# Adjacency tiles transposed by DMA instead of TensorE, column sums by later passes on ScalarE

## What is computed

```python
h = relu(layernorm(x));  mask = (adj > 0)
agg = mask @ h / max(sum(mask, axis=1), 1)
x = x + relu(concat(h @ W_self + b_self, agg @ W_nb + b_nb) @ W_comb + b_comb)
state = h = relu(layernorm(x));  A = adj as float
for _ in range(5):
    a_in  = A   @ (state @ in_W.T + in_b)
    a_out = A.T @ (state @ out_W.T + out_b)
    a = concat(a_in, a_out, state)
    r = sigmoid(a @ r_W.T + r_b);  z = sigmoid(a @ z_W.T + z_b)
    hh = tanh(concat(a_in, a_out, r * state) @ h_W.T + h_b)
    state = (1 - z) * state + z * hh
x = x + tanh(state @ o1_W.T + o1_b) @ o2_W.T + o2_b
```

## Time and profile before

| | us |
|---|---|
| median of 3 runs | 1241.61 (1240.56 to 1242.62) |
| the profiled execution | 1241.1 |
| its span, first to last instruction | 1239.3 |
| mean granted TensorE clock | 0.996 |
| TensorE matmuls busy | 1223.2 (99%) |
| TensorE weight loads busy | 591.1 (48%) |
| VectorE busy | 758.8 (61%) |
| ScalarE busy | 285.3 (23%) |
| GpSimd busy | 15.4 (1%) |
| DMA, mean rate | 146 GB/s |

### The profile page before, as it was taken

The page is one execution under the profiler, slowest core; times in us unless marked ns, Lnnn a source line. Parts: engine busy times, 40 slices in busy tenths (PEclk is TensorE's granted clock), DMA queues, the critical chain, the costliest instruction groups (busy, mean ns, idle before and its releaser), DMA issues.

```text
span 1239.3 us, 12868 instructions
## 1 busy us (share of the span) xinstructions
PE 1223.2 (99%) x4872; PEld 591.1 (48%) x4872; DVE 758.8 (61%) x1275; ACT 285.3 (23%) x556; POOL 15.4 (1%) x15
## 2 busy tenths in 40 slices
PE   8999999999899999999999999999999999999998
PEld 5666654444344444444444444444444444444445
DVE  6677734787884374387447348726834863662674
ACT  5756200022222021032112103301201330210122
POOL 4000000000000000000000000000000000000000
PEclk9999999999999999999999999999999999999999
DMA  9444643950007803810750570082075029016202
GB/s 328 161 162 171 250 174 141 342 237 0 1 0 287 290 1 111 305 60 0 281 194 1 198 277 1 34 335 106 1 276 199 1 102 345 29 56 216 89 1 68
DMA packets 44506, 180.61 MB, mean 146 GB/s; under 512 B 3489, under 2 KB 13474, under 8 KB 29346
## 3 DMA queue, kind: packets, MB, share of 16 engines
q1 hardware_dynamic: 43440, 176.04, 39.3%
q0 software_dynamic: 720, 3.67, 0.8%
q10 hardware_dynamic: 290, 0.14, 0.0%
HBM read 144.71 MB, written 35.13 MB: 145 GB/s over the span
## 4 chain that ended last, share of the span: by engine, by line
PE 88%; DVE 1%; issue 0%; DVEq 0%
PE bank L344 87%; PE bank L514 1%; DVE LF L1196 0%; DVE GR L1343 0%; PE bank L464 0%; DVE GR L1346 0%; DVE H L1092 0%; DVE AT L1049 0%; PE bank L412 0%; DVE DR L1060 0%; DVE fresh_S L1180 0%; DVE fresh_L L1178 0%; DVE res L1454 0%; DVE GR L1356 0%; DVE stat L987 0%
## 5 line engine op out<-in xcount | busy, mean ns | idle before, releaser
L344 PE MATMUL bank<-slot,LF 128*128 128x512 f16 x1792 | 389.5, 379 | 1.7 <-DVE LF L1196 1.7
L344 PEld LDWEIGHTS bank<-slot,LF 128*128 128x128 f16 x1792 | 175.2, 98 | 212.1 <-issue 4.5
L344 PE MATMUL bank<-X,W 128*128 128x512 f32 x384 | 180.5, 592 | 0.0
L344 PE MATMUL bank<-XT,W 128*128 128x512 f32 x288 | 135.3, 592 | 0.0
L344 PEld LDWEIGHTS bank<-X,W 128*128 128x128 f32 x384 | 72.5, 190 | 88.0 <-issue 86.9
L344 PE MATMUL bank<-AT,SN 128*128 (+1 forms) x256 | 97.1, 379 | 0.0
L344 PE MATMUL bank<-A,SN 128*128 (+1 forms) x256 | 97.0, 379 | 0.0
L1242 DVE TENSOR_TENSOR u_buf<-bank,m_buf 128x512 f32<-128x512 f32 x16 | 11.1, 691 | 134.0 <-PE bank L344 134.0
L344 PEld LDWEIGHTS bank<-XT,W 128*128 128x128 f32 x288 | 54.7, 190 | 68.9 <-issue 68.2
L764 ACT ACTIVATE m_buf<-bank 128x512 f32<-128x512 f32 x46 | 27.4, 595 | 232.0 <-PE bank L344 232.0
L344 PE MATMUL bank<-DR,work 128*128 128x512 f16 x256 | 67.1, 386 | 1.8 <-DVE DR L1060 1.6
(11 more groups left out here) (216 smaller groups left out, 1411.0 us busy)
## 6 DMA issues: line engine op xcount, KB each, us to landing
slot<-quad_d SPq DMA_DIRECT2D x112, 1024.0 KB, 5.3
WG<-in_adj SPq DMA_DIRECT2D x32, 512.0 KB, 4.2
quad_d<-AT SPq DMA_DIRECT2D x12, 1024.0 KB, 5.0
quad_d<-A SPq DMA_DIRECT2D x12, 1024.0 KB, 8.6
quad_d<-spare SPq DMA_DIRECT2D x4, 1024.0 KB, 4.0
SN<-in_x SPq DMA_DIRECT2D x2, 1024.0 KB, 10.5
x_d<-SN POOLq DMA_DIRECT2D x4, 512.0 KB, 3.2
x1o<-x_d SPq DMA_DIRECT2D x1, 2048.0 KB, 8.4
```

The costliest lines, as they stand in the source:

```text
L344: return pe.matmul(o, l, r, start=start, stop=stop, skip_group_check=again)
```

## The change

- TensorE's `turn_adj` and both `move_adj` are gone. SP turns a group of four tiles, a converted 512x512 part of A, with four DMA transposes of 128x512 from A to AT, group j behind its conversions and ahead of the load k = 2j+4. Four semaphores, used in turn, count their landing (TURNS).
- Group 4 waits for the last transpose of h and h's low half, since the buffer of h lies where AT is written; groups 8 and 12 wait for the setup and the store of the fused weights. These waits were ScalarE's and VectorE's.
- ScalarE converts further ahead of its loop index: five passes in four turns.
- Column sums: `column_sums` makes 64 passes on ScalarE over AT with accum_out into two scratch tiles, blocks 0 and 1 before out_pq(0), blocks 2 and 3 before out_pq(1).
- diag is split in two; the column diagonals are made after these passes, between VectorE's out_pq(1) and the first quad sums, in WG's place. spread_degrees(1) goes from the first spread to the middle of the third; out_degrees(1) goes between the two quad sums of A and AT, and the fourth spread waits for it.

```diff
+            def turn_adj(j):
+                b, c = j // 4, j % 4
+                sp.wait_ge(conv, 4 * (j + 1))
+                if j == 4:
+                    sp.wait_ge(hT_ready, NB)
+                    sp.wait_ge(h_lo, 4)
+                if j == 8:
+                    sp.wait_ge(setup_done, 1)
+                if j == 12:
+                    sp.wait_ge(st_fused, 16)
+                if j >= TURNS:
+                    sp.wait_ge(at_in[j % TURNS], 64 * (j // TURNS))
+                for q in range(BT):
+                    sp.dma_start_transpose(AT[:, b, BT * c:BT * c + BT, q * P:q * P + P],
+                                           A[:, c, BT * b + q, :]).then_inc(at_in[j % TURNS], 16)
+
             for k in range(2 * 4 * NB):
                 b, c, h = k // 8, k // 2 % 4, k % 2
                 if k >= RING:
                     sp.wait_ge(conv, 2 * (k - RING + 1))
+                if k >= 4 and k % 2 == 0:
+                    turn_adj(k // 2 - 2)
                 sp.dma_start(ring[:, k % RING, :, :], adj_v[b, c, h]).then_inc(ld_ring[k % RING], 16)
...
-                if i + LEAD < NT * NB:
-                    turn_adj(i + LEAD)
...
-            spread_degrees(1)
             spread(0, 11, NT - BT)
             pe.wait_ge(sn_hi, NB)
             pe.wait_ge(sn_lo, NB)
             spread(0, NT - BT, NT).then_inc(agg_done, 1)
+            spread(1, 0, NT).then_inc(agg_done, 1)
+            pe.wait_ge(pq_act, 2)
+            pe.wait_ge(pq_dve, 2)
+            spread(2, 0, 8)
+            pe.wait_ge(pq_act, 4)
+            pe.wait_ge(pq_dve, 4)
+            pe.wait_ge(diag_ready, 2)
+            spread_degrees(1)
+            spread(2, 8, NT).then_inc(agg_done, 1)
             pe.wait_ge(deg_out, 2 * NB)
-            for b in range(1, NB):
-                if b > 1:
-                    pe.wait_ge(pq_act, 2 * (b - 1))
-                    pe.wait_ge(pq_dve, 2 * (b - 1))
-                spread(b, 0, NT).then_inc(agg_done, 1)
+            spread(3, 0, NT).then_inc(agg_done, 1)
...
+            def column_sums(b):
+                for m in range(NT):
+                    i = NT * b + m
+                    if i >= 2:
+                        act.wait_ge(deg_sum, i - 1)
+                    copy(trash[i % 2], AT[:, b, m, :], accum_out=degT[:, m, b:b + 1]).then_inc(deg_sum, 1)
...
+            converted = 4
             for i in range(NT * NB):
-                k = 2 * (i // 4 + 1) + i % 4 // 2
-                if i == 0:
-                    move_adj(0)
-                if k < 8 * NB:
-                    convert(k, i % 2)
+                while converted < min(4 * NT, 5 + i + (i + 1) // 4):
+                    convert(converted // 2, converted % 2)
+                    converted += 1
...
             for b in range(NB):
+                if b < 2:
+                    column_sums(2 * b)
+                    column_sums(2 * b + 1)
                 out_pq(b)
...
             def make_mask(i):
                 b, m = i // NT, i % NT
-                if i % 2 == 0:
-                    dve.wait_ge(at_act, i // 2 + 1)
-                else:
-                    dve.wait_ge(at_dve, i // 2 + 1)
+                j = i // 4
+                if i % 4 == 0:
+                    dve.wait_ge(at_in[j % TURNS], 64 * (j // TURNS + 1))
...
             out_pq(0)
             out_pq(1)
+            dve.wait_ge(deg_sum, NT * NB)
+            link(v.tensor_reduce(degs[:, 1, :], degT[:, :, :], mybir.AxisListType.X, ALU.add))
+            diagonals(1)
             dve.wait_ge(quads_out, 16 * 12)
-            for x in range(2):
-                quad_sums(0, x)
+            quad_sums(0, 0)
+            dve.wait_ge(h2T_ready, NB)
+            out_degrees(1, degT_all)
+            dve.wait_ge(deg_out, 2 * NB)
+            quad_sums(0, 1)
```

More of the change, by code:

```diff
@@ L38 @@
 LEAD = 3
+TURNS = 4
 C_ID, C_ONE, C_END = 0, P, 2 * P
@@ L108, in graph_net @@
         first_XS = at("first_XS", 120 * KB, [P, 4, BN], FP32)
+        trash = [at(f"trash{i}", (202 + i) * KB, [P, BN], FP16)[:, :] for i in range(2)]
         x1o = at("x1o", 96 * KB, [P, NT, D], FP32)
@@ L129, in graph_net @@
         hi_lo = work[:, :].bitcast(FP16).rearrange("p (t s d) -> p t s d", t=NT, s=2)
-        diag = work[:, 8192:16384].bitcast(FP16).rearrange("p (w t n) -> p w t n", w=2, t=NT)
+        diag = [work[:, 8192:12288].bitcast(FP16).rearrange("p (t n) -> p t n", t=NT),
+                WG[:, :, :].rearrange("p k n -> p (k n)")[:, 0:1024].bitcast(FP16).rearrange("p (t n) -> p t n", t=NT)]
         idle16 = work[:, 0:2 * BN].bitcast(FP16)
@@ L180, in graph_net @@
         conv = sem("conv")
-        tr_ready = sem("tr_ready")
-        at_act, at_dve = sem("at_act"), sem("at_dve")
+        at_in = [sem(f"at_in{i}") for i in range(TURNS)]
+        deg_sum = sem("deg_sum")
         mask_ready, mask_used = sem("mask_ready"), sem("mask_used")
@@ L264, in _ @@
                     sp.wait_ge(conv, 2 * (k - RING + 1))
+                if k >= 4 and k % 2 == 0:
+                    turn_adj(k // 2 - 2)
                 sp.dma_start(ring[:, k % RING, :, :], adj_v[b, c, h]).then_inc(ld_ring[k % RING], 16)
-            sp.wait_ge(conv, 4 * NT)
-            sp.wait_ge(at_act, NT * NB // 2)
-            sp.wait_ge(at_dve, NT * NB // 2)
+            turn_adj(4 * NB - 2)
+            turn_adj(4 * NB - 1)
+            for i in range(TURNS):
+                sp.wait_ge(at_in[i], 64 * 4 * NB // TURNS)
             for p in range(2):
@@ L397, in biases @@
                 last.then_inc(setup_done, 1)
-            def turn_adj(i):
-                b, m = i // NT, i % NT
-                pe.wait_ge(conv, 4 * (4 * b + m // 4 + 1))
-                if i == 0:
[L403 to L407, removed]
-                    else:
[L409 to L413, removed]
             def mean_sum(i):
@@ L422, in mean_sum @@
                     pe.wait_ge(w12_out, 1)
+                    pe.wait_ge(id16_ready, 1)
                 if m == 0 and b > 0:
@@ L465, in turn_h2 @@
                 last.then_inc(h2T_ready, 1)
-            for i in range(LEAD):
-                turn_adj(i)
             biases()
@@ L505, in spread_degrees @@
                     last = mm(gate_bank[t // BT][:, (t % BT) * P:(t % BT) * P + P], one16[:, :],
-                              diag[:, w, t, :], True, True)
+                              diag[w][:, t, :], True, True)
                     if t % BT == BT - 1:
@@ L687, in _ @@
             pe.wait_ge(sn_lo, NB - 1)
-            pe.wait_ge(at_act, NT * NB // 2)
-            pe.wait_ge(at_dve, NT * NB // 2)
+            for i in range(TURNS):
+                pe.wait_ge(at_in[i], 64 * 4 * NB // TURNS)
             spread(0, 0, 2)
@@ L872, in _ @@
                 stage()
+            for i in range(TURNS):
+                act.wait_ge(at_in[i], 64 * 4 * NB // TURNS)
             def out_pq(b):
@@ L1114, in _ @@
                     sums(i // NT - 1)
-                if i % 2 == 1:
-                    move_adj(i)
                 if i in LOW_AT:
@@ L1141, in _, with diagonals @@
             dve.wait_ge(conv, 4 * NT)
-            dve.wait_ge(at_act, NT * NB // 2)
             v.tensor_reduce(degs[:, 0, :], degA[:, :, :], mybir.AxisListType.X, ALU.add)
-            v.tensor_reduce(degs[:, 1, :], degT[:, :, :], mybir.AxisListType.X, ALU.add)
             row_stats(range(BT * (NB - 1), NT), BT * (NB - 1))
             variance(range(BT * (NB - 1), NT), BT * (NB - 1))
-            for w in range(2):
+            def diagonals(w):
                 for t in range(NT):
-                    ins = v.tensor_scalar(diag[:, w, t, :], id16[:, :], degs[:, w, t:t + 1], None, ALU.mult)
-            ins.then_inc(diag_ready, 1)
+                    ins = v.tensor_scalar(diag[w][:, t, :], id16[:, :], degs[:, w, t:t + 1], None, ALU.mult)
+                ins.then_inc(diag_ready, 1)
+            diagonals(0)
             newton(BT, NB + 1)
@@ L1162, in _ @@
             turned(NB - 1)
-            dve.wait_ge(h2T_ready, NB)
-            out_degrees(1, degT_all)
-            dve.wait_ge(deg_out, 2 * NB)
             def out_pq(b):
```

21 lines of the change are left out of this document (removed).

## The result

The changed kernel takes 1268.4 us (median of 4 runs, 1266.51 to 1269.6), beside 1242.11 for the kernel before on the same chip: a ratio of 1.0212 (95% interval 1.0194 to 1.0229), so 26 us slower. The forecast was 5 us slower, 1246, with a range of 1230 to 1295. The sign was right, the size was not. The profiled execution has a span of 1267.8 us against 1239.3.

A forecast was written before the change was run, and what follows sets the result against it. TensorE, busy 99%, bounds the kernel. The adjacency stage gains 0.6 us net of stops, the lower clock costs 3.6 and the propagation stage 2.0: 5.0 us slower, 1246 us, range 1230 to 1295.

The forecast's parts named there:

- SP as the bound, slower by over 20 us: Rival for the adjacency stage: SP's transposes and loads outlast TensorE's work per group, slower by over 20 us; chance 0.22.
- What TensorE gives up: Adjacency stage: transposes cost TensorE 0.22 us each, 64 of them 14.1 us; a turn takes 0.97 us instead of 1.19.
- SP's price: Adjacency stage: one DMA transpose of 128x512 holds SP for 1.0 us, with ends of 0.37 and 9.3 us.
- The supply: Adjacency stage: a step with transposes takes 9.9 us, one without 5.9, so 5.3 us a group; TensorE averages 5.8.
- The threshold of the second rival: Adjacency stage: from about 1.4 us a transpose, SP takes 6.3 us a group against TensorE's 5.8; chance 0.22.
- The DMA engines are not the bound: Adjacency stage: 64 transposes at 0.45 us add 29 us to the DMA engines' 0.44 x 108.6 = 48 us.
- The stops: Adjacency stage: TensorE stands about 4 us at turns 30 and 46, together 8 us.
- The first block: Adjacency stage: four groups supplied at 5.3 us against TensorE's 4.8 lose 2 us.
- The lower clock: Adjacency stage: after each of two 4 us stops TensorE runs at a lower clock, costing 3.6 us together.
- A sign of being wrong: Adjacency stage: the prediction is wrong if the three-slot ring of loads runs dry where SP is idle; no size given.
- The propagation stage: Matmuls unchanged; later column sums and stores leave TensorE standing 2.0 us at the first gate group.
- The first rival: Adjacency stage: a transpose holds SP like a plain 128 KB load, 0.58 us or less; kernel 1234 us; chance 0.34.

The follow-up runs named there:

- the mix: Kernel before, with inserted groups of two adjacency loads plus transposes or plain copies, nothing waiting: 6.47 us a group with four transposes, 6.01 one wide, 3.77 copies.
- the two half versions: Kernel before with late column sums, every second group transposed by DMA, load first, buffers exchanged: 1265.9 us; with conversions further ahead and seven DMA groups: 1238.7 us.

## Why the prediction came out as it did

The direction was right, for a mechanism that the forecast had in part and priced too low. The 26 us lie above the 1240 to 1258 that the forecast gave itself; they fall under what it called "SP as the bound, slower by over 20 us", to which it gave 0.22. By its own steps:

- **What TensorE gives up** (0.22 us a tile): right. Two turns in the changed kernel without a stop start their matmuls at 159.64 and 160.62, 0.98 apart.
- **SP's price**, taken as 1.0 us: 1.27, inside the forecast's bounds. The load was taken at its row of before, 0.37; behind transposes it is 0.55 (1.09 for two, SP's timeline), and it lands after 5.1 us (median) instead of 4.2.
- **The supply**, 5.3 us a group: this is the term that was mis-sized. The formula comes near. With the measured values a step with transposes is 5.1 + 0.55 + 5.1 + 1.3 = 12.0 us, one without 6.95, and three groups in 19 us are 6.3 a group; SP's timeline shows 6.4 at best and 6.8 on average. That is above TensorE's 5.8, so nothing is ever caught up, and the stops are longer.
- **The threshold of the second rival** failed. It said that SP is the bound from 1.4 us a transpose, from 4 x 1.4 + 0.7. With two loads at 0.55 it is (5.8 - 1.1) / 4 = 1.18, and 1.27 is above it. What happened is the start of that rival; the forecast thought it 0.13 us away.
- **"The DMA engines are not the bound"** failed. By their share when nothing else runs, a transpose costs them 0.64 us, not the 0.45 of a load of the same size: 64 x 0.64 = 41 us beside 48 of loads, which would still fit into the stage. But between loads it costs more: the mix takes 6.01 us a group with a wide transpose and 3.77 with plain copies, and SP is then held for twice the time that the instruction takes alone. So I can't split the 16 us between plain copies and transposes into SP's part and the engines'; each alone gives a floor of 6.0 to 6.2 us a group.
- **The stops**: two of 4 us at masks 30 and 46 were forecast, 6.46 and 6.95 came. The start was to be 1.5 us late and was 3.0. The first block was to lose 2 us; three stops there (2.37, 2.41, 2.20) make 7.0. The 5.93 us at the first block's sums was missed. The prediction saw that at i = 16 ScalarE waits for these sums, but not that the sums then wait for a load (what it counts there as pieces 25 to 41 are passes, two to a piece): they stand behind a conversion of the piece that SP's hole at group 4 had delayed. With the buffers exchanged this stop is gone.
- **The lower clock** behind two stops, 3.6 us: it followed five of the seven. Of the 39.3 us that the stage lost (25.2 + 14.1), 30.5 are the seven stops and 1.4 are shorter waits for masks (3.1, where the kernel before has 1.7). The 7.4 left is about what the clock cost: from start to start, the work behind the five stops takes some 9.4 us more than the same work at the upper level, and the kernel before has 1.6 of that at the start of its own loop.
- **A sign of being wrong** that the prediction named, a ring that runs dry where SP is idle, came once: SP stood from 52.1 to 58.4 us for turn_h, and ScalarE's wait for the next piece was 9.2 us. The prediction had put this wait into the first block's 2 us.
- **The propagation stage** came out as worked out. Passes follow each other in 0.61 us (0.62 taken, 0.81 as the rival's), VectorE waits 1.48 us for the last of them (1.3 in the forecast's steps, 202.7 to 204.0), 16 diagonals take 2.69 (2.65), and VectorE waits 2.69 us for the stores of A's sums. The stop at the first gate group is 1.77 us, where 2.0 was forecast, and the version with the late sums alone shows 1.79. That its time is not longer by as much means that the 2.0 in the sum was right as a stop and too high as a price.

VectorE's timeline after shows these steps:

```profile
228.56 0.22 DVE L1391 TENSOR_REDUCE degs<-degT 128x16 f32<-128x64 f32 x1 [1.48 <-ACT trash L773]
228.81 2.69 DVE L1142 TENSOR_SCALAR WG<-id,degs 128x128 f16<-128x128 f16 x16
...
258.29 1.23 DVE L1213 TENSOR_TENSOR first_XT<-first_X,first_X 128x1024 f32<-128x1024 f32 x1 [2.69 <-DMA quad_d<-A]
```

The first rival (a transpose as cheap for SP as a load, 1234) is out by the 1.27 us, against 0.60 for a plain copy in the same form. The Trainium skill, page "Advanced Engine Details and Errata", section "X-Bar Transpose (TRN2)", has transpose DMAs as fast as regular ones; the runs here don't agree (0.64 against 0.39 us of the engines, and twice SP's time).

Where the expected gain went is thus known in its parts: 14.1 us were given up on TensorE as forecast. About 16 us were lost because these are transposes and not copies. About 24 more (10 over the kernel before, and the 14.1 that even the plain copies did not bring home) were lost to the order on SP, to latency and to the clock behind the stops, and up to 2 of them to the late sums. That the order on SP matters is shown in the changed kernel (10 us by the load ahead of the transposes), not apart beside plain copies. For latency the case is the two half versions, which differ mainly in how far the conversions lead: 1265.9 and 1238.7. They also differ in one DMA group (eight and seven) and in which group is the first, and I did not run these apart. That latency weighs as much when all groups go by DMA is not shown: all groups with the longer lead was not tried.

## What to carry to other kernels

Work that leaves a saturated TensorE for DMA is worth its length only if the producer runs ahead by issue plus landing (here 5.1 + 4.3 us, where a lead of two groups won and of one lost), and if the queue's and the engines' time for a group stay below TensorE's own. Compare the sum with the measured issue times of all that the queue carries, not with their times in an emptier kernel: 0.18 us on a load and 0.27 on a transpose turned "nearly hidden" into "never caught up". When the whole step doesn't fit into the free time of the DMA engines, move the part of it that does.

## What the runs showed of the hardware

- A DMA transpose holds SP for 1.25 to 1.34 us from 256 to 1024 columns of 128 partitions, but that is a floor and not a price: of 2048 columns it is 2.45 us alone, 4.7 to 5.1 between loads, and up to 5.9 and 7.9 in the two kernels that use it.
- By their share with nothing else under way, it costs the DMA engines 1.6 times a plain SBUF to SBUF copy with pieces of 256 bytes (0.64 and 0.39 us for 128 KB). Between loads the difference is larger: a group of 512 KB and two loads took 6.01 us with a wide transpose and 3.77 with plain copies. Six wide ones in a row (512 KB each in 2.45 us) ran at 214 GB/s.
- More transfers make the others late: loads of 512 KB landed after 4.2 us (median) at a mean share of 0.44 in the stage, 4.5 at 0.64 (half by DMA), 5.1 at 0.93 (all by DMA), and 7.0 when the transposes had SP's queue to themselves.
- A share of the engines near 1 is no measure of the room left: 266 GB/s at 0.99 in the version with plain copies, 375 at 1.07 in the mix with plain copies.
